# Bias of the second layer's expert down product: one f32r pass over a high and a low row in place of an fp32 product

## The chip, the cores and the metric

The kernel runs on one core of one Trainium2 chip. The metric is the device time of one execution in microseconds (us). Before the change the median of three runs is 3414.25 us (3413.76 to 3416.06).

The engines are called as in the profile: PE is TensorE (PEld its weight loads), DVE is VectorE, ACT is ScalarE, POOL is GpSimd, SP is the queue that issues the DMAs here.

## The reference, cut to what matters

A decoder of four layers; each has an attention, a cross attention and a feed-forward part with experts. The change lies in the feed-forward part of the second layer (L1_ffn). For each of 8 batches of 256 tokens (width 256), two of 8 experts are chosen, and every token of the batch goes through both:

```
top_scores, top_idx = jax.lax.top_k(pooled @ Wr, 2)
weights = jax.nn.softmax(top_scores, axis=-1)
W1s, b1s = (W1[top_idx], b1[top_idx])
W2s, b2s = (W2[top_idx], b2[top_idx])
h = jnp.einsum('btd,bkdf->bktf', x, W1s) + b1s[:, :, None, :]      # f = 1024
h = jax.nn.gelu(h, approximate=False)
y = jnp.einsum('bktf,bkfd->bktd', h, W2s) + b2s[:, :, None, :]     # d = 256
out = jnp.einsum('bk,bktd->btd', weights, y)
```

What the change touches is the term `b2s`, a row of 256 numbers that is added to each of the 256 tokens' rows of y.

## The kernel before

The function `experts_by_batch` computes this part. It works in 16 units, unit j being batch b = j // 2 and choice k = j % 2. Units with k = 0 are called even here, those with k = 1 odd. Products are made in f32r, a format in which a float is split into a high part (H) and the rest, the low part (L), and each product takes three passes: H·H, L·H, H·L.

In each unit:

- **PE** makes the up product, 48 passes of 256 columns into four PSUM banks (`("u", j, 0..3)`, line 2913). In an even unit it then transposes the next batch's tokens (line 2894, four fp32 products). Then it makes the bias product (line 2922): a row of ones (`g.ones`, one partition by 128) times the bias row (`g.bcast[0:1, ...]`, one partition by 256, read twice, so 512 columns), both fp32. This opens the accumulation in the bank of y. The down product follows (line 2931), 48 passes of 256 columns into the same bank.
- **ACT** applies the gelu to each up bank in place, with the bias b1 (`hidden(j, 0)` to `hidden(j, 3)`, line 2956). Between `hidden(j, 1)` and `hidden(j, 2)` it makes upH of the next unit's up weights (`up_high`, line 2942), in even units `x_high` behind `hidden(j, 2)`, and behind `hidden(j, 3)` it makes downH of the next unit (line 2948).
- **DVE** splits each of the four hidden pieces into hH (line 3043) and hL (line 3045). In even units it then normalizes the batch before (line 313, two TENSOR_SCALAR), adds the unit's y, weighted, to the tokens (line 3054), and in odd units takes the statistics of the finished batch (line 300 and on).
- **POOL** makes upL and then downL of the next unit's weights (lines 2993 and 2996), each a subtraction of 128x2048 elements that reads two SBUF tensors. `upL` of unit j + 1 waits for its `upH`, that is for ACT behind `hidden(j, 1)`. In even units POOL also makes the power for the layer norm.
- **SP** issues the loads: per unit the two weight halves, the column bias b1 and the row b2 (lines 2874 and 2876).

The order on each engine is the order in which the code is written; engines wait for one another on semaphores. There is no planner. A unit's own buffers (upH, upL, downH, downL) are doubled, by j % 2.

Of the kernel before, what the change touches and what calls it, by code (L numbers as in the profile page):

```python
# [13 lines left out]
ds = bass.ds  # L14
# [80 lines left out]
class Chip:  # L95


    def __init__(self, nc, ctx, dram):
# [112 lines left out]
        self.split_high, self.values_low = sig("narrow_weights_high"), sig("value_weights_low")  # L211
        self.xt_high, self.packed = sig("inputs_high"), sig("identity_packed")
        self.res_biased = sig("residual_biased")

    def expert_memory(self, scope, name):

# [2593 lines left out]
class Units:  # L2810


    def __init__(self, nc, g, scope):
        def sb(name, cols, dt=F32R):
            g.count += 1
            return scope.enter_context(nc.sbuf_tensor(f"{name}_{g.count}", [P, cols], dt))

        self.upH, self.upL = [sb("upH0", 2048), sb("upH1", 2048)], [sb("upL0", 2048), sb("upL1", 2048)]
        self.downH, self.downL = [sb("downH0", 2048), sb("downH1", 2048)], [sb("downL0", 2048), sb("downL1", 2048)]
        self.hH, self.hL = sb("hH", 2048), sb("hL", 2048)  # L2820


def experts_by_batch(nc, g, name, n, scope):
# [35 lines left out]
    with nc.Block() as block:  # L2859
        @block.sync  # L2860
        def _(sp):
            for j in range(NU):
                b, k = divmod(j, 2)
                e = sp.value_load(g.topi[0:1, b * E + k:b * E + k + 1], min_val=0, max_val=E - 1)
                if j >= 2:
                    src = g.dram[f"{name}.experts"][ds(e, 1), :, :].rearrange("a p c -> (a p) c")

                    split(sp, g.up_low, j - 2 + PIECES - 1)
                    sp.dma_start(raw[k][:, 0:2048], src[:, 0:2048]).then_inc(g.up_loaded[k].sem, 16)
                    split(sp, g.down_low, j - 2)  # L2870
                    sp.dma_start(raw[k][:, 2048:4096], src[:, 2048:4096]).then_inc(g.down_loaded[k].sem, 16)

                    filled(sp, ("y", j - 2))
                sp.dma_start(g.cols[:, k * 8:k * 8 + 8], g.dram[f"{name}.b1"][ds(e, 1), :, :].rearrange("a p c -> (a p) c"))\
                    .then_inc(g.half_loaded[k].sem, 16)
                sp.dma_start(g.bcast[0:1, k * D:(k + 1) * D], g.dram[f"{name}.b2"][ds(e, 1), :]).then_inc(g.half_loaded[k].sem, 16)
                if j == 1:
                    prefetch(nc, g, sp, n + 1)

        @block.tensor  # L2880
        def _(pe):
            def claim(key):
                pe.wait_ge(g.freed[u.bank(key)].sem, u.before(key, 0))
                return bank(key)

            def done(key, ins):
                ins.then_inc(g.filled[u.bank(key)].sem, 1)

            def transpose_x(b):
                to = claim(("X", b))  # L2890
                for k in range(2):
                    for t in range(2):
                        c0 = (2 * b + t) * D + k * P
                        mm = nc.tensor.transpose(to[:, k * S + t * P:k * S + (t + 1) * P], g.X[:, c0:c0 + P], g.ident[:, :])
                done(("X", b), mm)

            transpose_x(0)
            for j in range(NU):
                b, k = divmod(j, 2)
                if k == 0:  # L2900
                    pe.wait_ge(g.freed[u.bank(("X", b))].sem, u.taken(("X", b), 0))
                if j:
                    split(pe, g.up_low, j + PIECES - 1)
                for f2 in range(4):
                    if j == 0:
                        split(pe, g.up_low, f2)
                    to = claim(("u", j, f2))
                    for f in (2 * f2, 2 * f2 + 1):
                        at = 0
                        for kk in range(2):  # L2910
                            x0 = kk * T + b * S
                            for w_, x_ in ((m_.upH, g.xH), (m_.upH, g.xL), (m_.upL, g.xH)):
                                mm = nc.tensor.matmul(to[:, (f % 2) * S:(f % 2 + 1) * S], w_[j % 2][:, kk * 1024 + f * P:kk * 1024 + (f + 1) * P],
                                                      x_[:, x0:x0 + S], start=(at == 0), stop=(at == 5))
                                at += 1
                    done(("u", j, f2), mm)
                if k == 0 and b + 1 < B:
                    transpose_x(b + 1)
                split(pe, g.down_low, j)
                to = claim(("y", j))  # L2920
                loaded(pe, g.half_loaded, j, 32)
                nc.tensor.matmul(to[:, :].rearrange("p (t d) -> p t d", t=2), g.ones[:, :],
                                 g.bcast[0:1, k * D:(k + 1) * D].unsqueeze(1).to_broadcast([1, 2, D]), start=True, stop=False)
                for f in range(8):
                    if f % 2 == 0:

                        pe.wait_ge(g.freed[u.bank(("u", j, f // 2))].sem, u.taken(("u", j, f // 2), 0))
                    for t in range(2):
                        c0 = f * S + t * P
                        for at, (h_, w_) in enumerate(((m_.hH, m_.downH), (m_.hH, m_.downL), (m_.hL, m_.downH))):  # L2930
                            mm = nc.tensor.matmul(to[:, t * D:(t + 1) * D], h_[:, c0:c0 + P], w_[j % 2][:, f * D:(f + 1) * D],
                                                  start=False, stop=(f == 7 and t == 1 and at == 2))
                done(("y", j), mm)

        @block.scalar
        def _(act):
# [31 lines left out]
            down_high(0)  # L2968
            act.wait_ge(g.chosen_ready.sem, g.chosen_ready.base + 1)
            nc.scalar.activation(ex, ex, ACT.Exp).then_inc(g.act_step.sem, 1)  # L2970
            for j in range(NU):
                loaded(act, g.half_loaded, j, 32)
                hidden(j, 0)
                hidden(j, 1)
                if j + 1 < NU:
                    up_high(j + 1)
                hidden(j, 2)
                if j % 2 == 0 and j // 2 + 1 < B:
                    x_high(j // 2 + 1)
                hidden(j, 3)  # L2980
                if j + 1 < NU:
                    down_high(j + 1)

        @block.gpsimd
        def _(pool):
            def power(b):
                pool.wait_ge(g.var_ready.sem, g.var_ready.base + b + 1)
                nc.gpsimd.tensor_tensor(g.rstd[:, 2 * b:2 * b + 2], g.vare[:, 2 * b:2 * b + 2], g.mhalf[:, 0:2], ALU.pow).then_inc(g.rstd_ready.sem, 1)

            for j in range(NU):  # L2990
                if j:
                    split(pool, g.up_high, j + PIECES - 1)
                    nc.gpsimd.tensor_tensor(m_.upL[j % 2][:, :], raw[j % 2][:, 0:2048], m_.upH[j % 2][:, :].bitcast(F32), ALU.subtract)\
                        .then_inc(g.up_low.sem, 1)
                split(pool, g.down_high, j)
                nc.gpsimd.tensor_tensor(m_.downL[j % 2][:, :], raw[j % 2][:, 2048:4096], m_.downH[j % 2][:, :].bitcast(F32), ALU.subtract)\
                    .then_inc(g.down_low.sem, 1)
                b, k = divmod(j, 2)
                if k == 0 and b:
                    power(b - 1)  # L3000
            power(B - 1)

        @block.vector
        def _(dve):
# [30 lines left out]
            for j in range(NU):  # L3035
                b, k = divmod(j, 2)
                for f2 in range(4):
                    if f2 == 3 and k == 0 and b + 1 < B:
                        x_low(b + 1)
                    key = ("u", j, f2)  # L3040
                    at = slice(f2 * 512, (f2 + 1) * 512)
                    dve.wait_ge(g.h_raw.sem, g.h_raw.base + 4 * j + f2 + 1)
                    nc.vector.tensor_copy(m_.hH[:, at], bank(key)[:, :]).then_inc(g.h_high.sem, 1)
                    dve.wait_ge(g.h_high.sem, g.h_high.base + 4 * j + f2 + 1)
                    nc.vector.tensor_tensor(m_.hL[:, at], bank(key)[:, :], m_.hH[:, at].bitcast(F32), ALU.subtract)\
                        .then_inc(g.freed[u.bank(key)].sem, 1)
                if k == 0 and b:
                    dve.wait_ge(g.rstd_ready.sem, g.rstd_ready.base + b)
                    normalize_part2(nc, g, x_at(b - 1), 2, 2 * (b - 1))
# [24 lines left out]
    for k in range(2):  # L3074
        g.up_loaded[k].base += 16 * B
        g.down_loaded[k].base += 16 * B
        g.half_loaded[k].base += 32 * B
    g.var_ready.base += B
    g.rstd_ready.base += B

# [1118 lines left out]
```

## Time and profile before

| | us |
|---|---|
| median of three runs (lowest to highest) | 3414.25 (3413.76 to 3416.06) |
| span of the profiled execution | 3419.0 |
| PE busy in the span | 3115.7 (91%) |
| DVE busy | 1875.7 (55%) |
| ACT busy | 1705.1 (50%) |
| POOL busy | 1520.5 (44%) |

The profile is of one execution, whose span is 3419.0 us; the page gives no other time for it. Times within it are counted from the start of the span. The second layer's experts lie at about 1377 to 1594 us. Of matmuls the start is measured and the end is modelled, so in what follows the distance from one start to the next is what counts. A row of the timeline merges equal neighbours ("x2") and gives the start of the first, the time to the end of the last, and in brackets the idle time before it with what ended it.

### The profile page before, as it was taken

To read this page: it belongs to the slowest core of one execution; us is meant where nothing else is said; L and a number is where in the kernel's file an instruction comes from. 1 tells how busy PE (TensorE), PEld (TensorE's weight loads), DVE (VectorE), ACT (ScalarE), POOL (GpSimd) and SP (SyncE) were. 2 spreads that over 40 slices of the span, in tenths; PEclk is the share of its full clock that TensorE was granted. 3 is DMA by queue.
4 is the path that set the end of the run, shared out by engine and by line. 5 is a ranking of instruction groups with operands and counts; after the bars stand their busy time and mean duration, and the time that the engine had idled before them with its cause. 6 is when DMAs were issued, how large, how long until landed. Compare 5 with 4: busy or idle time off the path is not lost. (4 is left out here: it accounts for less than half of the span.)

```text
span 3419.0 us, 59989 instructions
## 1 busy us (share of the span) xinstructions
PE 3115.7 (91%) x23982; PEld 2628.8 (77%) x23993; DVE 1875.7 (55%) x3913; ACT 1705.1 (50%) x3695; POOL 1520.5 (44%) x1146
## 2 busy tenths in 40 slices
PE   6997999999698898998997989799997999889995
PEld 5776888888575565897665868678886888789995
DVE  4764222223566465776554754467775666565554
ACT  4763332332276554554654653356665666535553
POOL 0222344434212675674234651233334454539984
PEclk9998999999799999999998999899999999999998
DMA  1002000100000010442001010110001000036652
GB/s 65 3 11 79 19 19 19 38 1 1 23 3 23 1 50 1 149 168 75 3 3 43 8 50 1 39 50 1 1 1 38 6 6 1 26 115 217 223 181 74
DMA packets 49794, 156.96 MB, mean 46 GB/s; under 512 B 9322, under 2 KB 29438, under 8 KB 37104
## 3 DMA queue, kind: packets, MB, share of 16 engines
q1 hardware_dynamic: 45776, 142.90, 12.2%
q0 software_dynamic: 3744, 10.23, 1.0%
q8 instruction: 194, 3.18, 0.4%
q14 instruction: 80, 0.66, 0.1%
HBM read 142.06 MB, written 10.26 MB: 45 GB/s over the span
## 5 line engine op out<-in xcount | busy, mean ns | idle before, releaser
L1303 POOL TENSOR_TENSOR prob<-prob,inv 128x512 f32<-128x512 f32 x320 | 331.6, 1042 | 401.3 <-DVE inv L1355 391.8
L1193 ACT ACTIVATE prob<-banks,nmax 128x256 f32<-128x256 f32 x640 | 297.3, 474 | 155.1 <-DVE nmax L1349 155.0
L2682 POOL TENSOR_TENSOR hL<-product,hH 128x512 fp32r<-128x512 f32 x128 | 165.9, 1296 | 321.5 <-ACT hH L2629 321.5
L2288 DVE TENSOR_REDUCE nmax<-banks 128x4 f32<-128x1024 f32 (+1 forms) x192 | 217.5, 1133 | 153.7 <-PE banks L1870 85.9
L2727 DVE TENSOR_TENSOR product<-banks,silu 128x512 f32<-128x512 f32 x128 | 88.6, 692 | 388.6 <-PE banks L2553 333.4
L2621 ACT ACTIVATE silu<-banks 128x512 f32<-128x512 f32 x128 | 76.5, 598 | 367.6 <-PE banks L2553 367.6
L1349 DVE TENSOR_REDUCE nmax<-banks 128x2 f32<-128x512 f32 x320 | 215.4, 685 | 20.6 <-PE banks L1172 16.2
L2553 PE MATMUL banks<-xH,upH 128*128 128x512 f32 x512 | 202.1, 395 | 5.8 <-POOL upL L2669 5.8
L2553 PE MATMUL banks<-xL,upH 128*128 128x512 f32 x512 | 201.5, 394 | 0.0
L2553 PE MATMUL banks<-xH,upL 128*128 128x512 f32 x512 | 199.9, 390 | 0.0
L3364 ACT ACTIVATE banks<-banks 128x512 f32<-128x512 f32 x124 | 71.9, 584 | 213.9 <-PE banks L3308 186.8
L1093 PE MATMUL bank<-ident,prob 128*128 128x128 f32 x1280 | 167.8, 274 | 6.6 <-POOL prob L1303 6.6
L1093 PEld LDWEIGHTS bank<-ident,prob 128*128 128x128 f32 x1280 | 148.9, 141 | 21.8 <-issue 4.9
L2158 POOL TENSOR_TENSOR res<-res,bcast 128x512 f32<-128x512 f32 x16 | 21.4, 1337 | 313.7 <-DVE res L2356 313.7
L2105 ACT ACTIVATE probT<-banks 128x1024 f32<-128x1024 f32 (+1 forms) x129 | 123.2, 955 | 71.0 <-PE banks L1988 39.8
L3308 PE MATMUL banks<-xH,upH 128*128 128x256 f32 x496 | 142.7, 288 | 7.7 <-issue 7.7
L3308 PE MATMUL banks<-xH,upL 128*128 128x256 f32 x496 | 142.4, 287 | 6.7 <-issue 6.5
L3334 PE MATMUL bank<-downH,hH 128*128 128x256 f32 x496 | 143.7, 290 | 4.4 <-DVE hL L3648 4.3
L3308 PE MATMUL banks<-xL,upH 128*128 128x256 f32 x496 | 142.8, 288 | 3.2 <-issue 3.2
L2571 PE MATMUL bank<-downH,hL 128*128 128x256 f32 x512 | 144.9, 283 | 0.0
L2571 PE MATMUL bank<-downL,hH 128*128 128x256 f32 x512 | 144.8, 283 | 0.0
L2571 PE MATMUL bank<-downH,hH 128*128 128x256 f32 x512 | 144.4, 282 | 0.0
(617 smaller groups left out, 11026.6 us busy)
## 6 DMA issues: line engine op xcount, KB each, us to landing
W<-in_L_ffn_experts SPq DMA_DIRECT2D x80, 1024.0 KB, 5.4
W<-in_L_ffn_experts SPq DMA_DIRECT2D x8, 1536.0 KB, 7.9
slots_y<-W SPq DMA_DIRECT2D x23, 256.0 KB, 6.1
W<-strips SPq DMA_DIRECT2D x4, 768.0 KB, 7.5
W<-in_L_ffn_experts SPq DMA_DIRECT2D x9, 256.0 KB, 4.9
X<-in_x SPq DMA_DIRECT2D x1, 2048.0 KB, 8.3
cs<-in_ctxT SPq DMA_DIRECT2D x16, 128.0 KB, 2.3
W<-in_L_ffn_experts SPq DMA_DIRECT2D x1, 2048.0 KB, 7.6
```

The costliest lines, as they stand in the source:

```text
L1093: mm = nc.tensor.transpose(to[:, kt * S + qt * P:kt * S + (qt + 1) * P], m_.prob[p % 2][:, c0:c0 + P], ident[:, :])
L1193: ins = nc.scalar.activation(m_.prob[p % 2][:, e * 512 + j * S:e * 512 + (j + 1) * S], bank(key)[:, j * S:(j + 1) * S], ACT.Exp, bias=m_.n ...
L1303: nc.gpsimd.tensor_tensor(pr, pr, m_.inv[:, slot(p, e):slot(p, e) + 2].unsqueeze(2).to_broadcast([P, 2, S]), ALU.mult)\
L1349: nc.vector.tensor_reduce(m_.nmax[:, slot(p, e):slot(p, e) + 2], sc, AX.X, ALU.max, negate=True).then_inc(g.max_ready.sem, 1)
L2105: nc.scalar.activation(heads(m_.probT[(8 * b + i) % 3]), heads(g.pairs[1]), ACT.Exp)\
L2288: nc.vector.tensor_reduce(m_.nmax[b % 2][:, 2 * parts * i_:2 * parts * (i_ + 1)].rearrange("p (e q) -> p e q", e=2), scores.rearrange("p e ...
L2553: mm = nc.tensor.matmul(to[:, :], w_[e % 2][:, c0:c0 + P], x_[:, x0:x0 + 512], start=(at == 0), stop=(at == 5))
L2571: mm = nc.tensor.matmul(to, h_[:, c0:c0 + P], w_[e % 2][:, f * D:(f + 1) * D], start=(f == 0 and t % 2 == 0 and at == 0), stop=(f == 3 and ...
L2682: nc.gpsimd.tensor_tensor(m_.hL[:, at], m_.product[s % 2][:, :], m_.hH[:, at].bitcast(F32), ALU.subtract).then_inc(g.h_low.sem, 1)
L2727: nc.vector.tensor_tensor(m_.product[s % 2][:, :], bank(("u", s))[:, :], m_.silu[s % 2][:, :], ALU.mult)\
L3308: mm = nc.tensor.matmul(to[:, (f % 2) * S:(f % 2 + 1) * S], w_[w % 2][:, kk * 1024 + f * P:kk * 1024 + (f + 1) * P], x_[:, x0:x0 + S], sta ...
L3334: mm = nc.tensor.matmul(to[:, t * D:(t + 1) * D], h_[:, c0:c0 + P], w_[w % 2][:, f * D:(f + 1) * D], start=(f == 0 and t == 0 and at == 0) ...
```

## The change

The bias product becomes one f32r pass. Its stationary operand is a tile of ones with 128 rows (`m_.ones`), its moving operand a tile of 128 rows (`m_.b2[k]`) of which all are zero except row 0, the high part of the bias, and row 32, its low part. The sum over the rows is then high + low. To make these tiles:

- POOL clears the two tiles and fills the ones, once, ahead of its loop;
- SP loads the bias row twice, to partitions 0 and 32;
- ACT writes the high part to rows 0 and 32, by two copies of 1x256 between `hidden(j, 0)` and `hidden(j, 1)`;
- DVE subtracts, on row 32, the high part from the bias, behind the hL of piece 1;
- PE waits for DVE (`b2_low`) ahead of the bias product, where it had waited for the DMA.

```diff
@@ SP
-                sp.dma_start(g.bcast[0:1, k * D:(k + 1) * D], g.dram[f"{name}.b2"][ds(e, 1), :]).then_inc(g.half_loaded[k].sem, 16)
+                for row in (0, 32):
+                    sp.dma_start(g.bcast[row:row + 1, k * D:(k + 1) * D], g.dram[f"{name}.b2"][ds(e, 1), :]).then_inc(g.half_loaded[k].sem, 16)
@@ PE
                 split(pe, g.down_low, j)
                 to = claim(("y", j))
-                loaded(pe, g.half_loaded, j, 32)
-                nc.tensor.matmul(to[:, :].rearrange("p (t d) -> p t d", t=2), g.ones[:, :],
-                                 g.bcast[0:1, k * D:(k + 1) * D].unsqueeze(1).to_broadcast([1, 2, D]), start=True, stop=False)
+                split(pe, g.b2_low, j)
+                nc.tensor.matmul(to[:, :].rearrange("p (t d) -> p t d", t=2), m_.ones[:, :],
+                                 m_.b2[k][:, :].unsqueeze(1).to_broadcast([P, 2, D]), start=True, stop=False)
@@ ACT
+            act.wait_ge(g.b2_cleared.sem, g.b2_cleared.base + 1)
             for j in range(NU):
-                loaded(act, g.half_loaded, j, 32)
+                loaded(act, g.half_loaded, j, 48)
                 hidden(j, 0)
+                for row in (0, 32):
+                    ins = nc.scalar.activation(m_.b2[j % 2][row:row + 1, :], g.bcast[row:row + 1, (j % 2) * D:(j % 2 + 1) * D], ACT.Copy)
+                ins.then_inc(g.b2_high.sem, 1)
                 hidden(j, 1)
@@ POOL
+            nc.gpsimd.memset(m_.ones[:, :].bitcast(F32), 1.0)
+            nc.gpsimd.memset(m_.b2[0][:, :].bitcast(F32), 0.0)
+            nc.gpsimd.memset(m_.b2[1][:, :].bitcast(F32), 0.0).then_inc(g.b2_cleared.sem, 1)
@@ DVE
                     nc.vector.tensor_tensor(m_.hL[:, at], bank(key)[:, :], m_.hH[:, at].bitcast(F32), ALU.subtract)\
                         .then_inc(g.freed[u.bank(key)].sem, 1)
+                    if f2 == 1:
+                        split(dve, g.b2_high, j)
+                        nc.vector.tensor_tensor(m_.b2[k][32:33, :], g.bcast[32:33, k * D:(k + 1) * D], m_.b2[k][32:33, :].bitcast(F32), ALU.subtract)\
+                            .then_inc(g.b2_low.sem, 1)
```

How the engines' orders read, in two places. DVE in the middle of the stage, from an even unit's normalization (line 313, line 314 in the changed code) on; before:

```order
L313 TENSOR_SCALAR X<-X,meanvar,rstd 128x256 x2
L3054 SCALAR_TENSOR_TENSOR X<-bank,gates,X 128x256 x2
L3043 CAST hH<-banks 128x512
L3045 TENSOR_TENSOR hL<-banks,hH 128x512
L3043 CAST hH<-banks 128x512
L3045 TENSOR_TENSOR hL<-banks,hH 128x512
L3043 CAST hH<-banks 128x512
L3045 TENSOR_TENSOR hL<-banks,hH 128x512
```

And with the change (b_1_101 is the tile with the two bias rows, bcast the loaded bias):

```order
L314 TENSOR_SCALAR X<-X,meanvar,rstd 128x256 x2
L3069 SCALAR_TENSOR_TENSOR X<-bank,gates,X 128x256 x2
L3054 CAST hH<-banks 128x512
L3056 TENSOR_TENSOR hL<-banks,hH 128x512
L3054 CAST hH<-banks 128x512
L3056 TENSOR_TENSOR hL<-banks,hH 128x512
L3060 TENSOR_TENSOR b_1_101<-bcast,b_1_101 1x256
L3054 CAST hH<-banks 128x512
```

One instruction is added, behind the second hL of the unit; both of its inputs lie in SBUF, where hL has one input in PSUM (banks) and one in SBUF.

ACT in the first unit of the stage, with the change (line 2960 is the gelu, 2946 upH, 2965 xH):

```order
L2960 ACTIVATE banks<-banks,cols 128x256 x2
L2980 ACTIVATE b_0_100<-bcast 1x256 x2
L2960 ACTIVATE banks<-banks,cols 128x256 x2
L2946 ACTIVATE upH_90<-W 128x2048
L2960 ACTIVATE banks<-banks,cols 128x256 x2
L2965 ACTIVATE xH<-bank 128x2x256
```

The two copies of one row are new; they stand ahead of the second gelu pair and of upH, on which POOL waits.

## Rows read from the trace of the kernel before

**Rows 1.** Busy time of each engine over most of the stage.
```profile
core 0: us, PE busy (x) PEld busy (x) DVE busy (x) ACT busy (x) POOL busy (x), PEclk, DMA share, GB/s
1385.00:1590.00 205.00, 205.00 (x1577) 190.50 (x1576) 152.97 (x226) 107.56 (x165) 146.41 (x38) 1.00 0.41 148
```

**Rows 2.** The bias product's line: durations in ns, first and last start.
```profile
L2922 PE MATMUL bank<-bcast,ones x32: 587/640/692, 1389.1 to 1583.7; 1*128 1x512 f32 x32
```

**Rows 3.** PE's timeline, units 2 (even) and 3 (odd): start, us, instruction.
```profile
1408.82 0.28 PE L2913 MATMUL banks<-xH,upH 128*128 128x256 f32 x1
...
1414.46 0.28 PE L2913 MATMUL banks<-xH,upL 128*128 128x256 f32 x1
1414.58 0.60 PE L2894 MATMUL bank<-ident,X 128*128 128x128 f32 x4
1415.11 1.12 PE L2922 MATMUL bank<-bcast,ones 1*128 1x512 f32 x2
...
1416.38 0.28 PE L2931 MATMUL bank<-downL,hH 128*128 128x256 f32 x1
...
1422.02 0.28 PE L2913 MATMUL banks<-xH,upH 128*128 128x256 f32 x1
...
1427.66 0.28 PE L2913 MATMUL banks<-xH,upL 128*128 128x256 f32 x1
1427.87 1.12 PE L2922 MATMUL bank<-bcast,ones 1*128 1x512 f32 x2
...
1429.14 0.28 PE L2931 MATMUL bank<-downL,hH 128*128 128x256 f32 x1
```

**Rows 4.** ACT's timeline, the first two gelu pairs of unit 3.
```profile
1423.72 0.81 ACT L2956 ACTIVATE banks<-banks,cols 128x256 f32<-128x256 f32 x2 [5.37 <-PE banks L2913]
1425.10 0.81 ACT L2956 ACTIVATE banks<-banks,cols 128x256 f32<-128x256 f32 x2 [0.57 <-PE banks L2913]
```

**Rows 5.** A subtraction of 256 columns on DVE: busy us, mean ns.
```profile
L1372 DVE TENSOR_TENSOR qkL<-bank,qkH 128x256 fp32r<-128x256 f32 x96 | 39.7, 414 | 0.0
```

**Rows 6.** DVE's timeline: second hL of units 0 to 3, and what precedes unit 3's.
```profile
1390.53 0.69 DVE L3045 TENSOR_TENSOR hL<-banks,hH 128x512 fp32r<-128x512 f32 x1
...
1400.72 0.69 DVE L3045 TENSOR_TENSOR hL<-banks,hH 128x512 fp32r<-128x512 f32 x1
...
1413.47 0.69 DVE L3045 TENSOR_TENSOR hL<-banks,hH 128x512 fp32r<-128x512 f32 x1
...
1418.53 5.51 DVE L313 TENSOR_SCALAR X<-X,meanvar,rstd 128x256 f32<-128x256 f32 x2
1423.96 0.86 DVE L3054 SCALAR_TENSOR_TENSOR X<-bank,gates,X 128x256 f32<-128x256 f32 x2
...
1426.90 0.69 DVE L3045 TENSOR_TENSOR hL<-banks,hH 128x512 fp32r<-128x512 f32 x1
```

**Rows 7.** POOL's timeline in the same units.
```profile
1388.66 4.61 POOL L2993 TENSOR_TENSOR upL<-W,upH 128x2048 fp32r<-128x2048 f32 x1 [0.95 <-ACT upH L2942]
...
1401.86 4.62 POOL L2993 TENSOR_TENSOR upL<-W,upH 128x2048 fp32r<-128x2048 f32 x1 [3.99 <-ACT upH L2942]
...
1414.61 4.61 POOL L2993 TENSOR_TENSOR upL<-W,upH 128x2048 fp32r<-128x2048 f32 x1 [2.60 <-ACT upH L2942]
1419.18 4.70 POOL L2996 TENSOR_TENSOR downL<-W,downH 128x2048 fp32r<-128x2048 f32 x1
1427.82 4.62 POOL L2993 TENSOR_TENSOR upL<-W,upH 128x2048 fp32r<-128x2048 f32 x1 [3.94 <-ACT upH L2942]
```

**Rows 8.** DVE's timeline, another stage: one line, at two moments.
```profile
1195.19 1.84 DVE L831 TENSOR_TENSOR res<-res,bcast 128x512 f32<-128x512 f32 x1
...
1370.97 0.69 DVE L831 TENSOR_TENSOR res<-res,bcast 128x512 f32<-128x512 f32 x1
```

**Rows 9.** POOL's timeline at the first of these moments.
```profile
1194.59 1.89 POOL L736 TENSOR_TENSOR prob<-prob,inv 128x1024 f32<-128x1024 f32 x1 [7.92 <-DVE inv L810]
```

**Rows 10.** Busy time and granted clock about an idle gap of PE (columns as in rows 1).
```profile
2049.20:2052.60 3.40, 0.00 (x0) 0.00 (x0) 2.66 (x9) 1.86 (x4) 0.00 (x0) 0.81 0.00 0
2052.60:2058.00 5.40, 5.36 (x25) 5.32 (x26) 0.49 (x1) 0.00 (x0) 0.00 (x0) 0.50 0.00 0
2058.00:2060.00 2.00, 1.94 (x17) 1.27 (x15) 0.00 (x0) 1.27 (x3) 0.00 (x0) 0.96 0.00 0
```

More of the change, by code:

```diff
@@ L213, in __init__ @@
         self.res_biased = sig("residual_biased")
+        self.b2_cleared, self.b2_high, self.b2_low = sig("down_bias_cleared"), sig("down_bias_high"), sig("down_bias_low")
     def expert_memory(self, scope, name):
@@ L2820, in __init__ @@
         self.hH, self.hL = sb("hH", 2048), sb("hL", 2048)
+        self.ones = sb("ones_rows", P)
+        self.b2 = [sb("b2_0", D), sb("b2_1", D)]
 def experts_by_batch(nc, g, name, n, scope):
@@ L3076, in experts_by_batch @@
         g.down_loaded[k].base += 16 * B
-        g.half_loaded[k].base += 32 * B
+        g.half_loaded[k].base += 48 * B
+    g.b2_cleared.base += 1
+    for sig in (g.b2_high, g.b2_low):
+        sig.base += NU
     g.var_ready.base += B
```

## The prediction

> **What bounds the kernel now.** I read the busy times over the stage first. From 1385 to 1590 us PE is busy for all of the 205 us, at the full granted clock (1.00, the level of 2.4 GHz), while DVE is busy 153, ACT 108 and POOL 146 us [rows 1]. So the stage ends when PE has issued its last product, and a microsecond taken off PE's stream is a microsecond of the kernel as long as nobody else comes late. Then I read the line of the bias product and PE's timeline. The bias is 32 instructions for 16 units, two each [rows 2], as an fp32 product is made in two passes. The passes of the up and down products start 0.12 us apart (from 1408.82 to 1414.46 are 47 distances, [rows 3]). Last come the timelines of ACT, DVE and POOL about the places where the new row has to be made, since PE will wait for it. Those decide this case.
>
> **The gain on PE.** In odd unit 3 the last up pass starts at 1427.66, the second down pass at 1429.14: 1.48 us for what would be two distances of 0.12 without the bias [rows 3]. One f32r pass of 512 columns should take twice the distance of a 256 column pass, 0.24 at most, and there is no change of format around it, so 0.12 + 0.22 + 0.12 = 0.46: a gain of 1.0 us. In even unit 2 the fp32 transposes stand ahead. From the start of the bias (1415.11) to the second down pass (1416.38) are 1.27 us [rows 3]; with f32r I put 0.33 and leave 0.1 for the change of format, which now lies ahead of the bias: 0.42, a gain of 0.85 (0.65 if the change of format costs the full 0.3). With 8 units of each kind that is 8 x 1.0 + 8 x 0.85 = 14.8 us, if the bias row is there in time each time. The ones tile's 128 rows in place of one are not in this: the weight load lies beside the pass before it.
>
> **What the row's making costs by itself.** ACT's two copies of 1x256 each cost about what half a gelu pair costs, 0.4 us [rows 4], between zero and 0.8 for both. In unit 3 ACT sat idle 0.57 us between the two pairs, so nearly all of it is covered and `hidden(j, 1)` comes at most 0.1 to 0.25 later; gelu, upH and POOL's upL shift with it. The subtraction on DVE is 414 ns for 128x256 elsewhere [rows 5]; I take 0.35. Three POOL memsets and the extra DMA lie where POOL and SP have nothing due: POOL's first work of the stage follows ACT's downH, and SP's row is asked for a whole unit ahead. Zero.
>
> **Where the subtraction stands.** It runs behind the second hL. In even unit 2 that hL starts at 1413.47 and ends at 1414.16, so the row would be ready at about 1414.5, ahead of the bias at 1415.11; POOL's upL begins at 1414.61, behind it [rows 3, 6, 7]. Good. In odd unit 1 hL starts at 1400.72, the subtraction at 1401.4 and is done by 1401.75, just as PE would want it; POOL's upL begins at 1401.86 [rows 6, 7]. Good, with about half a microsecond between the two starts, and both hang on the same gelu, so ACT's copies shift both alike.
>
> In odd unit 3 (and 5, 7, ..., 15) DVE is late by its own work. The normalization of the batch before takes 5.51 us for two small instructions, until 1424.04, which is the end of POOL's downL (1419.18 + 4.70 = 1423.88) plus 0.16 [rows 6, 7]. Behind it stand the two y additions and four halves of splitting, so the second hL starts at 1426.90 and ends at 1427.59. That chain starts at the even unit's second gelu, and nothing in the change shortens it. But PE and POOL come earlier here: with the 0.85 gained in unit 2, up pass 1422.02 moves to 1421.17, the bias is wanted at 1426.9 and POOL's upL for unit 4 moves from 1427.82 to 1426.97. The subtraction comes to its place at 1427.5, half a microsecond **behind** POOL's start, where before the gain it would have been 0.3 ahead.
>
> **What happens when they meet.** The subtraction reads two SBUF tensors, and the trace shows such a DVE instruction beside a POOL one. Line 831 takes 0.69 us with POOL idle. At 1195.19 it takes 1.84, to 1197.03: POOL's instruction ran from 1194.59 to 1196.48, and DVE ended 0.55 behind it [rows 8, 9]. It was not slowed, it stood until POOL was done. hL reads one input from PSUM and keeps its 0.69 beside POOL (1426.90 and all others).
> The Trainium skill says the same of this pairing (SBUF — State Buffer, "Who interferes with whom"): a VectorE instruction with two SBUF inputs contends with a GpSimd instruction that reads SBUF, and the later one blocks in full. By that rule the trace agrees, 1.84 against 0.69 us; a reading by which short one-row instructions slip through finds no support there.
>
> So in unit 3 the subtraction stands until 1426.97 + 4.62 = 1431.59 [rows 7] and ends at about 1431.95. PE starts the bias at 1432.0 and the second down pass at 1432.4, in place of 1429.14: **3.25 us lost**. The second half of hL, 2.6 us later than the subtraction, is at 1434.6, ahead of its products. Everything behind (up of unit 4, statistics, POOL) hangs on PE, so the next pair of units repeats this from its own start. It holds for units 3, 5, ..., 13, six times. In unit 15 there is no unit 16 whose upL POOL could make: there only DVE's lateness counts, the row is ready at about 1428.0 in unit 3's times, the bias starts there, and 1.0 + 0.85 of the pair shrinks to 0.4 gained.
>
> Unit 0 meets it too. Its second hL ends at 1391.22 and POOL's upL runs from 1388.66 for 4.61 us [rows 6, 7], from about 1388.95 with ACT's copies, to 1393.57. Row ready 1393.9, second down pass 1394.35. The bias started at 1389.1 [rows 2] and the second down pass 1.27 behind it, 1390.4. **3.95 us lost.** Unit 1 gains 0.95.
>
> **The clock.** Each of these stalls leaves PE idle for 5 us (unit 3: 1426.9 to 1432.0; unit 0: 4.8). About an idle gap of 3.4 us elsewhere the granted clock falls to 0.50, the level of 1.2 GHz, and the 25 products of the next 5.4 us run at it, 0.216 us apart, before it is back [rows 10]. At the full clock they are 0.12 apart, so such a gap costs 25 x 0.096 = 2.4; I take 2.3 behind each of seven stalls, between 0 and 2.8.
>
> **The sum.** Unit 0: 3.95 + 2.3 = 6.25. Unit 1: -0.95. Six pairs with a stall: 6 x (3.25 + 2.3) = 33.3. Last pair: -0.4. Total +38.2 us. The profiled span of 3419.0 becomes 3457.2; it stands 4.75 above the median of the runs, and on that median the time is 3414.25 + 38.2 = 3452.5 us. Most of the price lies in the stalls, so bounds are 0 and 2.8 for the clock (+22.1 to +41.7).
>
> **The rivals.**
> - *DVE is first.* If the subtraction gets in ahead of POOL's upL in the odd units, for instance as the even units gain under 0.3 us and POOL starts no earlier, POOL stands 0.3 us and nothing more. PE waits for DVE until about 1428.0 and its second down pass starts at 1428.35: 0.8 gained a pair. Six times 0.8 and 0.4 and 0.95, against 6.25 in unit 0: -6.15 + 6.25 = 0, 3414 us. If a one-row subtraction is not blocked at all, unit 0 costs 1.5 in place of 6.25: 3409 us. For it speaks that the distance is half a microsecond; against it, that both ends of the distance hang on rows that repeat to 0.02 us, and that the gain in even units is twice what is needed. It is the case that is not slower. 9 in 100.
> - *The gain comes through.* The row is ready in time everywhere (a DVE chain that moves with PE): -14.8 us, 3399.5. Against it stands the normalization, bound to POOL's downL and not to PE, and unit 0, whose hL ends 2 us behind the bias [rows 3, 6]. 4 in 100.
> - *The clock holds.* The stalls come but PE keeps its clock: +22.1, 3436 us. The rows speak against it. 9 in 100.
> - *POOL is first everywhere.* Also in units 1, 2, 4, ... the half microsecond goes the other way: each then stalls some 4 us, and with the clock about 6, in 8 more units: about +85, 3500 us. 6 in 100.
>
> **How the numbers follow.** The forecast has 72 in 100. Its own range goes from +30 to +46 (clock, ACT's shift, one more unit blocked). Taking in the case of the clock that holds, the range is 3433 to 3464; it leaves out 19 in 100. A measurement of this kernel tells 0.2%, 6.8 us, from no change. Slower: 72 + 9 + 6 = 87 in 100; within 0.2%: the 9 in which DVE is first; faster: 4.
>
> **What would show it.** In the changed profile the new subtraction has two sorts of durations: about 0.35 us in units 1, 2, 4, ..., and 4 to 5 us in units 3, 5, ..., 13, 2 to 3 in unit 0, each ending just behind an upL of POOL. PE's idle time ahead of the bias is put down to that subtraction, 5 us at a time, seven times, and the granted clock shows 0.5 behind each. The bias product is 16 instructions that take about 0.24 us from start to start. If the subtraction never exceeds 0.7 us the central step is wrong, and if it does but PE's idle time is not at the bias product, the step by which PE wants the row at once is.

## The result, and the profile after

| | before | changed |
|---|---|---|
| median, us (lowest to highest) | 3415.15 (3413.76 to 3419.5, 4 runs) | 3443.49 (3441.92 to 3446.44, 4 runs) |
| ratio (95% interval) | 1 | 1.0087 (1.0072 to 1.0101) |
| profiled span | 3419.0 | 3444.3 |
| stage, first up product to last down product | 209.5 (1380.5 to 1590.0) | 246.8 (1375.5 to 1622.3) |

The median before counts the profiled execution too. The change made the kernel slower, by 28 us of 3415. Run once more beside the kernel before (15 runs of it) the ratio was 1.0098 (1.0082 to 1.0114). The forecast of 3452.5 us was 9 us too high, inside its range. The stage is read from one profiled execution of each kernel: it grew by 37.3 us, while the spans of the same two executions differ by 25.3.

The line of the new subtraction first, with durations in ns and who waited:

```profile
L3060 DVE TENSOR_TENSOR b<-bcast,b x16: 415/416/4174, 1386.3 to 1615.8; 1x256 fp32r<-1x256 f32 x16
...
  PE bank L2926: 37.8, 10
```

A one-row subtraction takes 0.42 us in nine units and 2.73 to 4.17 us in the other seven. PE waited 37.8 us for it, in ten units; seven of these waits are the long ones. Now PE's timeline in units 2 and 3, which answers to [rows 3] (start, us, instruction, idle time before it):

```profile
1409.75 0.28 PE L2917 MATMUL banks<-xH,upH 128*128 128x256 f32 x1
...
1416.20 0.47 PE L2926 MATMUL bank<-b,ones_rows 128*128 128x512 f32 x1
1416.50 0.28 PE L2935 MATMUL bank<-downH,hH 128*128 128x256 f32 x1
...
1422.26 0.28 PE L2917 MATMUL banks<-xH,upH 128*128 128x256 f32 x1
...
1427.90 0.28 PE L2917 MATMUL banks<-xH,upL 128*128 128x256 f32 x1
1433.30 0.77 PE L2926 MATMUL bank<-b,ones_rows 128*128 128x512 f32 x1 [5.12 <-DVE b L3060]
1433.86 0.42 PE L2935 MATMUL bank<-downH,hH 128*128 128x256 f32 x1
...
1441.76 0.28 PE L2917 MATMUL banks<-xH,upH 128*128 128x256 f32 x1
```

From its first up product to that of the next unit, unit 2 is shorter than before (12.5 us where it was 13.2), unit 3 is longer (19.5 us where it was 12.76). The two engines behind that wait, DVE and then POOL (answers to [rows 6, 7]):

```profile
1419.78 5.61 DVE L314 TENSOR_SCALAR X<-X,meanvar,rstd 128x256 f32<-128x256 f32 x2
1425.31 0.86 DVE L3069 SCALAR_TENSOR_TENSOR X<-bank,gates,X 128x256 f32<-128x256 f32 x2
...
1428.26 0.69 DVE L3056 TENSOR_TENSOR hL<-banks,hH 128x512 fp32r<-128x512 f32 x1
1428.98 4.17 DVE L3060 TENSOR_TENSOR b<-bcast,b 1x256 fp32r<-1x256 f32 x1
1433.18 0.69 DVE L3054 CAST hH<-banks 128x512 fp32r<-128x512 f32 x1
```

```profile
1415.87 4.70 POOL L3004 TENSOR_TENSOR upL<-W,upH 128x2048 fp32r<-128x2048 f32 x1 [2.13 <-ACT upH L2946]
1420.52 4.72 POOL L3007 TENSOR_TENSOR downL<-W,downH 128x2048 fp32r<-128x2048 f32 x1
1428.38 4.50 POOL L3004 TENSOR_TENSOR upL<-W,upH 128x2048 fp32r<-128x2048 f32 x1 [3.14 <-ACT upH L2946]
```

The subtraction starts 0.60 us behind POOL's upL and ends 0.27 behind its end (1433.15 against 1432.88). The windows of the stall, the 4.7 us behind it and the 9 after those (columns as in [rows 1]):

```profile
1428.20:1433.30 5.10, 0.00 (x0) 0.03 (x1) 5.00 (x4) 3.35 (x6) 4.92 (x2) 0.87 0.66 278
1433.30:1438.00 4.70, 4.70 (x21) 4.61 (x22) 2.56 (x4) 0.00 (x0) 4.29 (x1) 0.50 0.00 0
1438.00:1447.00 9.00, 9.00 (x74) 9.00 (x74) 4.56 (x12) 3.48 (x7) 0.70 (x1) 0.96 0.20 49
```

Behind this stall PE works at a granted clock of 0.50, the level of 1.2 GHz. Behind the later ones it does so for less time: over the 7.4 us from the bias product on, the mean granted clock is 0.63 in unit 3, then 0.70, 0.74, 0.76, 0.77 and 0.78 in units 5 to 13. All starts of the stage, put together per unit from such timelines, in us (a unit goes from its first up product to that of the next, its down part begins at its first down product):

| | unit 0 | unit 1 | even 2 to 12 | odd 3 to 13 | unit 14 | stage |
|---|---|---|---|---|---|---|
| before | 15.61 | 12.76 | 13.2 | 12.76 | 12.76 | 209.5 |
| changed | 22.04 | 12.20 | 12.51, then 12.21 | 19.51 falling to 18.57 | 12.20 | 246.8 |
| of which the down part, before | 5.87 | 5.86 | 5.86 | 5.86 | 5.86 | |
| the down part, changed | 7.79 | 5.75 | 5.76 | 7.90 falling to 6.96 | 5.75 | |

Unit 15, up to its last down product, takes 13.47 us where it took 12.64.

### The profile page after: what moved, and what is told of

It is laid out like the page before. It is cut to its first block and busy times, and to the rows that moved or that the text cites. A ratio compares the mean times of both kernels' runs of the same rounds, so it can differ in the third digit from the quotient of the medians.

```text
span 3444.3 us, 60051 instructions
## 1 busy us (share of the span) xinstructions
PE 3108.1 (90%) x23977; PEld 2634.1 (76%) x23977; DVE 1907.3 (55%) x3929; ACT 1718.2 (50%) x3727; POOL 1521.9 (44%) x1149
```

## The experiments

Stages and units below are read as in that table, each from one profile. Absolute times differ between comparisons (the kernel before has medians of 3389.9, 3414.8 and 3412.5 us in the three), so each kernel is judged by its ratio to the kernel before, run beside it. In the cuts of code `...` stands for what is left out.

**The subtraction on POOL.**

```diff
+            def bias_low(j):
+                split(pool, g.down_low, j)
+                if j % 2 == 0 and j:
+                    pool.wait_ge(g.rstd_ready.sem, g.rstd_ready.base + j // 2)
+                split(pool, g.b2_high, j)
+                nc.gpsimd.tensor_tensor(m_.b2[j % 2][32:33, :], g.bcast[32:33, ...], m_.b2[j % 2][32:33, :].bitcast(F32), ALU.subtract)\
+                    .then_inc(g.b2_low.sem, 1)
             for j in range(NU):
                 if j:
+                    bias_low(j - 1)
+                    split(pool, g.b2_low, j - 1)
                     split(pool, g.up_high, j + PIECES - 1)
...
-                    if f2 == 1:
-                        split(dve, g.b2_high, j)
-                        nc.vector.tensor_tensor(m_.b2[k][32:33, :], ...)
```

> The subtraction that makes the low row goes from DVE to POOL, ahead of its upL; all else as in the changed kernel. Lock theory (the price of the change is DVE's subtraction standing behind POOL's upL): POOL has 2 to 4 us idle there, the row is ready about 1 us before PE wants it in odd units, no stall, the clock stays at 1.00. Gain on PE of 8 x 1.0 + 8 x 0.85, less 0.5 in unit 0 where PE then waits for hL: about -14 us against the kernel before, 3401 us; stage 195 us against 209.5 before and 246.8 in the changed kernel. Rival (the wait of PE for any late row, or ACT's copies, is what costs, whichever engine subtracts): little of the 28 us comes back, 3430 us or more.

Measured: ratio 0.9952 (0.9938 to 0.9966), stage 195.0 us. Its units are 15.97, 11.75, then 12.17 to 12.19 (even) and 11.75 (odd). POOL and PE in unit 3:

```profile
1416.98 0.73 POOL L3006 TENSOR_TENSOR b<-bcast,b 1x256 fp32r<-1x256 f32 x1
1419.75 4.65 POOL L3014 TENSOR_TENSOR upL<-W,upH 128x2048 fp32r<-128x2048 f32 x1 [2.04 <-ACT upH L2946]
```

```profile
1419.33 0.40 PE L2926 MATMUL bank<-b,ones_rows 128*128 128x512 f32 x1
```

The row is ready at 1417.7, 1.6 us ahead of PE, without idle time at the bias product. The theory holds to its numbers; the rival falls, since copies, DMA, wait and product are all still there. Run once more, in another comparison:

> The version with the subtraction on POOL once more, beside the kernel before on one chip: ratio about 0.995 as in its first run (stage 195.0 us against 209.5 or 215.4), if that gain is not a matter of that chip.

Measured: ratio 0.9952 (0.9935 to 0.9968), stage 195.0 us. This version beats both kernels, the one before by 16 us by the ratio of each of the two comparisons.

**The subtraction one piece earlier.**

```diff
-                    if f2 == 1:
+                    if f2 == 0:
                         split(dve, g.b2_high, j)
```

> The subtraction stays on DVE but stands behind the first hL of the unit, 1.3 us earlier than in the changed kernel. Lock theory: in odd units it now comes to its turn at 1426.3 in the trace of before, ahead of POOL's upL (1427.0), so the six stalls of 5 us vanish; in unit 0 POOL's upL has already begun at 1384.3 in the trace of the changed kernel while the first hL starts about there, so that one stall mostly stays (duration 1 to 4 us). Total about -8 us against before, 3407 us; sixteen durations, fifteen of them near 0.42 us. Rival (a price of the instruction itself wherever it stands, or of PE's wait): stays near the changed kernel, 3440 us.

Measured: ratio 0.9987 (0.9970 to 1.0003), stage 204.7 us, so 4.8 less than before where 8 were expected. Of the sixteen durations fifteen are 0.42 us; unit 0's is 4.03. DVE and POOL in unit 3:

```profile
1424.27 0.41 DVE L3060 TENSOR_TENSOR b<-bcast,b 1x256 fp32r<-1x256 f32 x1
```

```profile
1424.79 4.64 POOL L3004 TENSOR_TENSOR upL<-W,upH 128x2048 fp32r<-128x2048 f32 x1 [2.94 <-ACT upH L2946]
```

Half a microsecond ahead of POOL in place of 0.6 behind it, and the stall of 5 us is gone. The missing 3 us: odd units take 12.2 to 12.3 us, as the bias product still starts 0.4 to 0.5 us later in the unit than with the row made on POOL, and unit 0 keeps all of its loss (21.96 us). The interval of the ratio holds 1, so this version isn't shown to beat the kernel before.

**The fp32 product with the new wait.**

```diff
                 split(pe, g.b2_low, j)
-                nc.tensor.matmul(to[:, :]..., m_.ones[:, :], m_.b2[k][:, :].unsqueeze(1).to_broadcast([P, 2, D]), start=True, stop=False)
+                nc.tensor.matmul(to[:, :]..., g.ones[:, :], g.bcast[0:1, k * D:(k + 1) * D].unsqueeze(1).to_broadcast([1, 2, D]), start=True, stop=False)
```

> The bias product is the fp32 one of before, but PE waits for the low row as in the changed kernel; copies and subtraction stay. Theory that the gain on PE itself pulls POOL's upL ahead of DVE: without the 0.85 us gained in even units POOL starts 0.3 us behind the subtraction in odd units, so these do not stall (each subtraction about 0.42 us, PE waits 0.1 to 0.3 us); unit 0 stalls as before. About +6 to +9 us against before, 3421 to 3424 us. Rival (the stall in odd units does not depend on what PE gained): six stalls with the fp32 product behind them, +37 us or more, 3450 us.

Measured: ratio 1.0056 (1.0034 to 1.0078), stage 223.2 us. All subtractions but unit 0's (2.74) take 0.42 us. Even units take 13.2, odd ones 13.36 us. The stalls of the odd units are gone with the gain that caused them. The sum was 13.7 us and not 6 to 9: six odd units cost 0.6 each (I had 0.1 to 0.3), unit 0 costs 7.3, units 1 and 14 cost 0.25 each, and unit 15, which I had left out, costs 2.3.

**Only the odd units f32r.**

```diff
+                ones_, row_, n_ = (m_.ones[:, :], m_.b2[k][:, :], P) if k else (g.ones[:, :], g.bcast[0:1, 0:D], 1)
+                nc.tensor.matmul(to[:, :]..., ones_, row_.unsqueeze(1).to_broadcast([n_, 2, D]), start=True, stop=False)
```

> The f32r bias in odd units only; even units make the fp32 product of before, so that PE gains nothing there. Copies, subtraction and waits as in the changed kernel. Race theory (the gain of 1 us in the even unit pulls POOL's upL ahead of DVE's subtraction in the next odd one): even units 13.2 us, odd units 12.5 us with a wait of 0.6 us, all subtractions but that of unit 0 at 0.42 us; +6 us against before, ratio 1.002, although seven of the eight products that are changed are those that stalled. Rival (odd units stall whatever the even ones do): 6 stalls of 5 us and the clock, +37 us.

Measured: ratio 1.0010 (0.9999 to 1.0022), stage 215.3 us; even units 13.2, odd 12.55. DVE and POOL in unit 3:

```profile
1424.46 0.41 DVE L3060 TENSOR_TENSOR b<-bcast,b 1x256 fp32r<-1x256 f32 x1
```

```profile
1424.64 4.72 POOL L3004 TENSOR_TENSOR upL<-W,upH 128x2048 fp32r<-128x2048 f32 x1 [3.93 <-ACT upH L2946]
```

DVE is first by 0.18 us. The seven stalls of the changed kernel shrink to one although all odd units are as changed. What is left is unit 0 (22.9 us, 7.3 more than before); the other units together gain 1.5. So it is the even unit's gain of 1 us that brings POOL ahead of DVE in the next odd unit.

**POOL's upL in eight pieces.**

```diff
-                    nc.gpsimd.tensor_tensor(m_.upL[j % 2][:, :], raw[j % 2][:, 0:2048], m_.upH[j % 2][:, :].bitcast(F32), ALU.subtract)\
-                        .then_inc(g.up_low.sem, 1)
+                    for c in range(0, 2048, 256):
+                        ins = nc.gpsimd.tensor_tensor(m_.upL[j % 2][:, c:c + 256], raw[j % 2][:, c:c + 256], m_.upH[j % 2][:, c:c + 256].bitcast(F32), ALU.subtract)
+                    ins.then_inc(g.up_low.sem, 1)
```

> POOL makes each upL behind the first unit in 8 pieces of 256 columns in place of one of 2048; all else as in the changed kernel. Lock theory (DVE stands for the whole POOL instruction it meets): it now meets one of some 0.65 us and gets in behind it, so durations of 3.9 us fall to about 1 us, PE's wait to 1.0 to 1.5 us, under what makes the clock fall. Six odd units then cost nothing or gain a little, total -5 to +2 us against before, about 3413 us. Rival (POOL keeps the port over a row of instructions, or has it as long as it has work): the durations stay at 4 us, 3440 us.

Measured: ratio 1.0013 (0.9997 to 1.0028), stage 213.4 us. The subtraction's line:

```profile
L3061 DVE TENSOR_TENSOR b<-bcast,b x16: 414/416/972, 1380.4 to 1576.5; 1x256 fp32r<-1x256 f32 x16
...
  PE bank L2926: 14.2, 14
```

The longest stand is 0.97 us, so DVE gets in behind the one short instruction that it meets. The eight pieces take 5.6 to 5.8 us where one took 4.6. PE's 14.2 us of waiting are now spread over 14 units. The stage is 3.9 us longer than before, where -5 to +2 was expected: PE waits 3.7 us in unit 0 and 0.2 to 1.6 in most others, and the later waits I had priced at nothing. Why the row is so late in even units shows ahead of unit 2's pieces (DVE, then POOL):

```profile
1404.58 1.95 DVE L308 TENSOR_SCALAR vare<-meanvar 128x2 f32<-128x2 f32 x1
```

```profile
1401.84 4.66 POOL L3008 TENSOR_TENSOR downL<-W,downH 128x2048 fp32r<-128x2048 f32 x1
```

An operation of 128x2 that takes 0.17 us in the same place before took 1.95 us, until 0.03 behind POOL's downL, and what DVE does behind it in the unit is late. In the even units 2 to 14 the length of this operation goes with how far the bias product lies behind the unit's first up product: 6.46 us at 0.98, 7.31 at 1.84, 7.94 at 1.95. So with the pieces, which delay downL, this other long instruction of POOL met another one of DVE's.

**PE kept busy while it waits.**

```diff
+                for _ in range(42 if j == 0 or (k and 0 < b < B - 1) else 0):
+                    nc.tensor.matmul(to[:, 0:D], m_.upH[j % 2][:, 0:P], g.xH[:, b * S:(b + 1) * S], start=True, stop=True)
                 split(pe, g.b2_low, j)
```

> The changed kernel, but PE makes 42 idle products of 256 columns (5 us, into the bank that the bias product then opens) ahead of its wait in units 0, 3, 5, ..., 13. Clock theory: the waits stay as long (bias 11.05 us behind the unit's first up product), but the granted clock stays at 1.00 and the down products behind them take 5.76 us in place of 7.8 in unit 0 and 7.0 to 7.9 in the odd units: 2.0 + 6 x 1.5 = 11 us less than the changed kernel, stage 236 us, ratio to before 1.0075. Rival (the down products behind a stall are slow for another reason, late hL or downL): nothing comes back, ratio as in the changed kernel.

Measured: ratio 1.0073 (1.0055 to 1.0091), stage 234.5 us against 246.8. The medians, 3438.7 against 3448.2 us for the changed kernel in the same comparison, differ by less, and the two intervals overlap. The wait and the down products of unit 3:

```profile
1423.30:1428.50 5.20, 5.20 (x44) 5.07 (x43) 5.13 (x3) 3.62 (x6) 4.76 (x2) 1.00 0.67 284
1428.60:1434.20 5.60, 5.47 (x44) 5.42 (x45) 2.75 (x5) 0.00 (x0) 4.59 (x1) 1.00 0.01 3
```

Every down part is 5.75 or 5.76 us, and in the odd units that stall the bias still comes 11.1 us behind the first up product. That is the share of the clock: 12.3 of the stage's 37.3 us. The other 25.0 are the stalls less the gain.

**The change and the kernel before once more, on one chip.**

> The changed kernel once more, beside the kernel before on the same chip. In its first profile the stage grew by 37.3 us while the medians differ by 28.3. If the difference is that of two chips or moments, the ratio here is 1.0109 (37 us); if something outside the stage really got shorter with the change, it stays near 1.0085 (28 us).

> The kernel before, for a profile on the same chip as the others of this call: stage of 209.5 us from the first up product to the last down product, as in its first profile, and the rest of the program as in the changed kernel's profile of this call, if the change touches nothing outside the stage.

Measured: ratio 1.0098, between the two answers, and its interval (1.0082 to 1.0114) holds both, so it doesn't choose. The change's stage is 246.8 us again, the same unit by unit to 0.1 us. But the stage of the kernel **before** is 215.3 us this time: its unit 0 took 21.41 us in place of 15.60. DVE, POOL and PE there:

```profile
1376.13 4.50 DVE L3033 COPY gates<-small 128x8 f32<-128x8 f32 x1
```

```profile
1376.10 4.50 POOL L2993 TENSOR_TENSOR upL<-W,upH 128x2048 fp32r<-128x2048 f32 x1 [0.47 <-ACT upH L2942]
```

```profile
1382.21 0.58 PE L2931 MATMUL bank<-downH,hH 128*128 128x256 f32 x1 [4.56 <-DVE hL L3045]
```

A copy of 8 columns, 0.03 us behind POOL's upL, took 4.5 us and ended 0.03 behind its end; hL came late, PE waited 4.56 us for it, and its down part took 7.55 us in place of 5.87. In the first profile POOL had sat idle 0.95 us ahead of this upL [rows 7], and the copy was through. So one of the two profiles of the kernel before has this stall; how many of its executions have it isn't known. It occurs in none of the eleven profiles with ACT's two copies.

**Parts alone: copies only, then copies and subtraction without PE's wait.** Both keep the fp32 product and the wait for the DMA; the first has no subtraction either.

```diff
-                split(pe, g.b2_low, j)
+                loaded(pe, g.half_loaded, j, 48)
...
-                    if f2 == 1:
-                        split(dve, g.b2_high, j)
-                        nc.vector.tensor_tensor(m_.b2[k][32:33, :], ...)
```

> The kernel before with only ACT's two copies per unit, the second DMA of the row and POOL's three memsets; fp32 product, wait for the DMA, no subtraction. Theory: the copies delay POOL's first upL by some 0.5 us, so DVE's two-port copy to the gates in unit 0 is always ahead of it, and unit 0 takes 15.6 us, never 21.4; nothing else changes, stage 209.5 us, ratio 0.998 to 1.000. Rival (ACT's copies cost something of their own in each unit): odd units over 12.8 or even ones over 13.2 us, ratio over 1.002.

Measured: ratio 1.0006 (0.9992 to 1.0019), stage 209.5 us, every unit as in the first profile of before. The copies, the second DMA and the memsets cost the stage nothing. POOL's first upL has 1.48 us of idle time ahead of it here. The ratio was expected at 0.998 to 1.000, for a kernel that never has the stall of unit 0; the measured one lies just above, and its interval can't tell whether such a gain is there.

> The same, and DVE makes its subtraction too, but PE waits only for the DMA. Theory that the lock costs only through PE's wait: the subtraction of unit 0 still stands for 2.7 us, which makes the third and fourth hL late and costs PE 2 to 3 us there; all other units as before, stage 212 us, ratio about 1.000. Rival (DVE's standing still is itself what costs the time): unit 0 loses 6 us or more, ratio over 1.002.

Measured: ratio 1.0015 (1.0002 to 1.0027), stage 213.5 us. Unit 0 takes 19.6 us, 4.0 more than before (2.5 expected; PE waits 2.24 us for hL, and the down products behind that are partly at the lower clock), all others as before. So a blocked DVE costs 4 us in unit 0 even where PE doesn't wait for the row, which lies between the theory's 2 to 3 and the rival's 6. Of the odd units this run says nothing: without the gain on PE their subtractions all take 0.42 us.

## Why the prediction was right, step by step

- **What bounds.** PE, as read. With the row in time on POOL, what was taken off PE's stream came off the stage (195.0 against 209.5 us) and, with 16 us, off the median.
- **The gain on PE.** With the row in time on POOL, 1.0 us in odd units as predicted (11.75 against 12.76), 1.0 in even ones where 0.85 was chosen. In the changed kernel unit 2 alone gained only 0.7: its line 308 took 0.97 us in place of 0.17, behind POOL's downL.
- **Two-input subtraction and POOL.** Right in place and size. Predicted 0.5 us behind POOL in odd units, found 0.60; predicted to end 0.35 behind POOL, found 0.27. It stood in unit 0 and in units 3, 5, ..., 13, and nowhere else. Two readings beside it were less sound. The hL at 1426.90 is given as one that runs beside POOL, but POOL sat idle then; the row that shows it is the hL at 1390.53, 0.69 us while upL ran from 1388.66 [rows 6, 7]. And it isn't only instructions with two inputs that stand: the copy of 128x8 above has one, and so have the TENSOR_SCALARs of line 308 and of the normalization, whose 5.51 us the prediction did tie to POOL's downL.
- **Unit 0.** +6.44 us, predicted +6.25.
- **The six pairs.** Odd units 18.9 us in the mean, +6.1; with the even unit's gain 5.2 a pair, predicted 5.55. The term that was mis-sized is the clock: its 2.3 us per stall was right in unit 0 and unit 3 (2.2 and 2.3 us more than with PE kept busy), but it fell to 1.4 by unit 13, 1.7 in the mean of the six. The rest without it, predicted at +22.1, was +25.0 with PE kept busy.
- **Last pair and unit 1.** Unit 1 gained 0.56 in place of 0.95: its bias starts 6.14 us behind its first up product, and 5.76 with the row made on POOL. The last pair lost 0.3 in place of gaining 0.4: unit 14 gained 0.56, unit 15 lost 0.83, with the bias 7.54 us behind its first up product where 6.8 follows from the prediction's times for unit 3. The 0.4 doesn't agree with its own rivals, either: there the same working gives 0.8 a pair.
- **The sum.** The stage grew by 37.3 us, predicted 38.2. That the agreement is so close is partly luck, small errors of both signs. The upper bound of the range, +50 us, isn't reached by the terms given for it, which end at +46.
- **From the stage to the median.** This step failed: I set the whole of 38.2 on the median, and 28.3 came (33 in the second comparison). Shown: the kernel before can have a stall in unit 0, worth 5.8 us of its stage, that its first profile didn't have, so the change replaces a loss that is there part of the time. Not settled: outside the stage the changed kernel's profiled execution took about 12 us less than that of the kernel before, both times. From the last down product of the stage to the last product of the fourth layer's experts it is 1804.0 and 1801.0 us with the change, 1811.1 and 1814.3 without. The granted clock over the first 240 us of it was 0.91 and 0.91, against 0.91 and 0.89. A later start of these stages is not what does it: with the subtraction on POOL, where they start earlier than before, the second run took 1801.5 us for them, against 1810.5 for the copies alone in the same comparison. Whether it is chance was not tried.

## What to carry to other kernels

Before an operation is added to DVE whose result the bounding engine waits for, list what POOL runs at that moment **after** the change, with the gain already taken off: here 1 us won on PE moved POOL's 4.6 us instruction ahead of a 0.4 us one, and made a good product change a loss. What helped here was to give the operation to POOL itself, ahead of its long instruction and in time in which it sat idle (0.72 to 0.74 us each time, no stall), or, for the odd units, to place it on DVE half a microsecond ahead of it. Cutting the long instruction in pieces shortened the stand to 0.97 us, but POOL's next long instruction then met another of DVE's. And a stall of 5 us of PE should be priced with the slower clock behind it, a third of the stage's loss in this case.

## What the runs showed of the hardware that was not expected

- A DVE copy of 128x8, 0.17 us when free, takes 4.50 us when it is issued 0.03 us behind a POOL subtraction of 128x2048. A margin of tens of nanoseconds goes with 4.5 us of that copy, and with 5.8 us of the stage between two profiles of one kernel.
- The same one-row subtraction takes 0.73 us on POOL and 0.42 on DVE.
- The cost of the clock behind equal stalls isn't constant: the down part behind a wait of 5.1 us took 7.90, 7.46, 7.22, 7.08, 7.02 and 6.96 us in units 3, 5, ..., 13, the same in two runs to 0.02 us.
